# Attention's next queries: low part on GpSimd instead of VectorE, norm and rounding at other exponents on ScalarE

## The chip, the cores and the metric

The kernel runs on one core of one Trainium2 chip. The metric is the device time of one execution in microseconds (us). The change touches one of the kernel's stages, an attention over 32 tiles of queries.

## The reference, cut to what matters

The reference is a block of four layers on x (16 batches, 256 rows, 512 columns). The change lies in the third, a cross attention with keys and values from the context ctx_2048:

```
x = x + jnp.tanh(g_xattn[1]) * _L1_xattn_ref(_layernorm(x, axis=-1), ctx_2048, ctx_2048)

def _L1_xattn_ref(q, k, v):
    N_HEAD = 8
    b, d, m = q.shape
    qh = q.reshape(b * h, d // h, m)
    kh = k.reshape(b * h, d // h, -1)
    vh = v.reshape(b * h, c // h, -1)
    qk = jnp.einsum('bdm,bdn->bmn', qh, kh) * scale
    sm = jax.nn.softmax(qk, axis=-1)
    ret = jnp.einsum('bmn,bcn->bcm', sm, vh)
    return ret.reshape(b, c, m)
```

With d = 256 and 8 heads, each head has 32 features; scores are 512 x 512 per head. The query is the layer norm of a row of x, (x - mean) / sqrt(var + eps). Before this layer stand a convolution and a mixture of experts, behind it a second mixture of experts with a router that picks 2 of 8 experts.

## The kernel before, in words

The attention is cut into 32 units (UNITS). A unit is half a batch: 128 features, that is 4 heads (NH) of 32, against 512 positions. One pass of `body(j, i, u)` on each engine handles unit j. `unit_loop` (L1114) writes the first four and the last four units out and puts the others in a hardware loop of 4 units a trip; each engine has its own loop, and only semaphores tie them together.

For a unit, TensorE does each score twice. `score` (L1349) makes them with queries in the rows (into pA), and VectorE's `reduce` (L1710) takes the negated row maximum from them (into low). GpSimd's `halves` (L1291 to L1297) splits low into two parts, TensorE transposes them (`maxima`, L1368), ScalarE copies the result to tops (`keep`, L1561), and SyncE writes tops as two further rows of the query operand (`shift`, L1178 to L1182). `second` (L1371, matmul L1377) then makes the scores transposed with the maximum already subtracted, one 128 x 512 tile at a time, into pB, and ScalarE takes the exponent of each tile (L1608) into pt. A unit has 16 such tiles, so 16 score matmuls and 16 exponents. `values` (L1387) multiplies pt by the values, `sums` (L1400) adds up the denominators, for which GpSimd has added three of the four slices of pt (L1311, L1316).

The score matmuls of `second` use two banks in turn: `bank` picks one of pB's two, `place` numbers the tiles and leaves one place free for the transposes behind TURN = 10, and a tile waits until the one two places ahead has been read by ScalarE:

```
            def place(j, s, h):
                return NH * s + h + (1 if NH * s + h >= TURN and exists(j + 1) else 0)
            def second(j, u, s, h):
                n = place(j, s, h)
                if s == 0 and h == 0:
                    pe.wait_ge(s_md, 32 * j + 32)
                wait(pe, s_exp, made(j, n - 2))
```

The operands are kept in two parts, a rounded high one and a low one, the rest. For units ahead of time the kernel also makes the queries: ScalarE's `query` (L1590) applies the norm to a tile of x and writes nextq, `query_high` (L1596) rounds it into nexth, `query_low` (L1720, on VectorE) writes the difference nextl. SyncE's `store_query` (L1163, L1164) puts both parts in device memory, from where `load` (L1159) fetches them as operands of a later unit. In body j it is the query of unit j + 4. The query stands behind the exponent number 1 (counted from 0), the rounding behind number 5, the low part behind VectorE's reduce of beat 9. `query` waits until the low part before it is made, `query_high` until the stores before it have landed, `store_query` for the low part, and `load` of unit j + 3 for the stores of its query.

Other work of a unit: `add_row` (L1302) and `refine` (L1277 to L1286) on GpSimd, `scale` (L1716) and `measure` (L1724, L1727) on VectorE, `logarithm`, `inverse`, `root` and `norm` (L1566, L1571, L1577 and L1580, L1586) on ScalarE.

Of the kernel before, what the change touches and what calls it, by code (L numbers as in the profile page):

```python
# [6 lines left out]
F32R = mybir.dt.float32r  # L7
I32 = mybir.dt.int32
U32 = mybir.dt.uint32
ALU = mybir.AluOpType  # L10
# [14 lines left out]
NH, HD1 = 4, 32  # L25
# [46 lines left out]
def _build(nc, a, out, whole):  # L72
# [952 lines left out]
    with ExitStack() as st:  # L1025
# [85 lines left out]
        KHu, KLu, QHu, QLu = units(KH), units(KL), units(QH), units(QL)  # L1111
        QHr, QLr = (d.rearrange("b (th p) c -> (b th) p c", p=P) for d in (QH, QL))

        def unit_loop(eng, body):  # L1114

            trips = UNITS // TRIP
            for u in range(TRIP):
                body(u, 0, u)
            with eng.Fori(1, trips - 1) as i:
                for u in range(TRIP):  # L1120
                    body(i * TRIP + u, i, u)
            for u in range(TRIP):
                body(UNITS - TRIP + u, trips - 1, u)

        def exists(j):
            return not isinstance(j, int) or 0 <= j < UNITS
# [28 lines left out]
        def _(sp):  # L1155
            def load(j, u):
                for dst, src in ((ks[u][0:HD1], KHu[j]), (ks[u][HD1:2 * HD1], KLu[j]), (ks[u][2 * HD1:NS], KHu[j]),
                                 (qs[u][0:HD1], QHu[j]), (qs[u][HD1:2 * HD1], QHu[j]), (qs[u][2 * HD1:NS], QLu[j])):
                    sp.dma_start(dst, src).then_inc(s_ld[u], 16)  # L1159
# [24 lines left out]
            def body(j, i, u):  # L1184
                before, n = exists(j - 1), (u + TRIP - 1) % TRIP
                if exists(j + 3):
                    if before:
                        sp.wait_ge(s_b, made(j - 1, place(j - 1, CB - 1, NH - 1)))
                        sp.sem_inc(s_go, 1)
                        sp.wait_ge(s_qs, 32 * j)  # L1190
                    load(j + 3, n)
                if exists(j + 1):
                    shift(j + 1, (u + 1) % TRIP)
                if exists(j + 4):
                    store_query(j + 4)
                if exists(j - 2):
                    store(j - 2, (u + 2) % TRIP)
                if exists(j + 3):
                    if before:
                        sp.wait_ge(s_av, CB * j)  # L1200
                    load_values(j + 3, n)
                if exists(j - 4):
                    store_normed(j - 4)
# [42 lines left out]
        def _(pool):  # L1246
# [52 lines left out]
            def add_row(j):  # L1299
# [2 lines left out]
                pool.tensor_tensor(row, row, att, ALU.add).then_inc(s_x3, 1)  # L1302
                pool.wait_ge(s_x3, j + 1)

            def body(j, i, u):
                if exists(j + 1):
                    halves(j + 1, (u + 1) % TRIP)
                pool.wait_ge(s_exp, made(j, place(j, 1, NH - 1)))
                wait(pool, s_sum, 2 * j - 1)
                for n in range(2):  # L1310
                    pool.tensor_tensor(part_sum[:, 2 * n:2 * n + 2], pt[0][:, 2 * n:2 * n + 2], pt[1][:, 2 * n:2 * n + 2],  # L1311
                                       ALU.add).then_inc(s_add, 1)
                    pool.wait_ge(s_add, 4 * j + n + 1)
                pool.wait_ge(s_exp, made(j, place(j, 2, NH - 1)))
                for n in range(2):
                    pool.tensor_tensor(part_sum[:, 2 * n:2 * n + 2], part_sum[:, 2 * n:2 * n + 2], pt[2][:, 2 * n:2 * n + 2],  # L1316
                                       ALU.add).then_inc(s_add, 1)
                    pool.wait_ge(s_add, 4 * j + n + 3)
                if exists(j - 1):
                    add_row(j - 1)  # L1320
                if exists(j - 3):
                    refine(j - 3, (u + 1) % TRIP)

            halves(0, 0)
            constants()
            unit_loop(pool, body)
            add_row(UNITS - 1)
            for u in range(1, TRIP):
                refine(UNITS - TRIP + u, u)
# [223 lines left out]
        def _(act):  # L1553
# [44 lines left out]
            def body(j, i, u):  # L1598
                for s in range(CB):
# [5 lines left out]
                    for h in range(NH):  # L1605
                        n = place(j, s, h)
                        act.wait_ge(s_b, made(j, n))
                        act.activation(pt[s][:, h, :], bank(u, n), ACT.Exp, scale=SCALE1).then_inc(s_exp, 1)  # L1608
                        if NH * s + h == 1 and exists(j + 4):
                            query(j + 4)  # L1610
                        if NH * s + h == 5 and exists(j + 4):
                            query_high(j + 4)
                        if NH * s + h == 3 and exists(j - 3):
                            root(j - 3, (u + 1) % TRIP, 0)
                        if NH * s + h == 4 and exists(j - 3):
# [7 lines left out]
                        if NH * s + h == TURN + 2 and exists(j - 1):  # L1623
                            inverse(j - 1)

            keep(0, pB[1], 1)
            unit_loop(act, body)

            def columns(n):
                act.wait_ge(s_t, n + 1)  # L1630
# [71 lines left out]
        def _(dve):  # L1702
# [12 lines left out]
                wait(dve, s_x3, j)  # L1715
                dve.scalar_tensor_tensor(att, pO[u % 2], gates[:, 1:2], inv, ALU.mult, ALU.mult).then_inc(s_att, 1)  # L1716

            def query_low(j):
                dve.wait_ge(s_q, 2 * j - 6)
                dve.tensor_tensor(nextl.bitcast(F32R), nextq, nexth, ALU.subtract).then_inc(s_ql, 1)  # L1720

            def measure(j, u):
                dve.wait_ge(s_x3, j + 1)
                dve.bn_stats(stats6[:, u % 2, :], ap(XN, j * ROW, [[1, C]])).then_inc(s_bn, 1)  # L1724
# [6 lines left out]
            def body(j, i, u):  # L1731
                for beat in range(1, TILES, 2):
                    to = ahead(j, i, u, beat)
                    reduce(*to[:3], to[3] // 2)
                    if beat == 9 and exists(j + 4):
                        query_low(j + 4)
                    if beat == 5 and exists(j - 2):
                        measure(j - 2, (u + 2) % TRIP)
                    if beat == 13 and exists(j - 1):
                        scale(j - 1, u - 1)  # L1740
# [205 lines left out]
```

## Time and profile before

| what | value |
| --- | --- |
| median of 3 runs | 1681.53 us (1680.91 to 1683.77) |
| profiled execution | 1682.86 us |
| its span, first to last instruction | 1681.1 us |
| TensorE busy in the span | 1531.7 us, 91% |
| VectorE, ScalarE, GpSimd busy | 1250.4, 967.7 and 1021.2 us |
| the attention's 512 exponents (L1608) | 290.0 us busy |
| the 28 low parts (L1720) | first at 593.5, last at 1015.4 us |
| granted TensorE clock, mean | 0.951 |

Busy time is that of one engine; engines run beside each other, so the figures do not add up to the span. The span is a little shorter than the execution's time, since the latter has what lies around the first and the last instruction. A granted clock of 1.00 is TensorE's 2.4 GHz, 0.50 is 1.2 GHz.

### The profile page before, as it was taken

Reading aid. Unit: us, or ns where it says so; the run is one execution under the profiler, and the core shown is the slowest. Engines: PE = TensorE matmul, PEld = TensorE weight load, DVE = VectorE, ACT = ScalarE, POOL = GpSimd, SP = SyncE. Lnnn points to the kernel's source line nnn. Section 1 sums busy time; section 2 is a strip of 40 time slices with the busy share of each in tenths; the row PEclk is TensorE's granted clock in tenths of the full one; section 3 lists DMA queues with packets and bytes.
Section 4 is the critical chain, followed back from the end, with each engine's and each line's share of the span. In section 5 each row is a group of like instructions: output and inputs, shape, how many; then the busy total and the mean of one; then the engine's idle time right before and its main releaser. Section 6 shows DMA issues by size and latency. Waiting matters only on the chain.

```text
span 1681.1 us, 28191 instructions
## 1 busy us (share of the span) xinstructions
PE 1531.7 (91%) x8674; PEld 1054.5 (63%) x8674; DVE 1250.4 (74%) x1795; ACT 967.7 (58%) x1523; POOL 1021.2 (61%) x965
## 2 busy tenths in 40 slices
PE   5999999996676599999999999886999999999996
PEld 4677777775442244444444444366998999999985
DVE  7688888888538578888888887245677777777774
ACT  6333333325422167777778777745677676777763
POOL 4788888874203367887787787700355555555553
PEclk9999999998789589999999999987999999999998
DMA  6344444427452847677776764292244444444443
GB/s 248 114 139 139 143 140 142 137 102 202 100 154 72 194 118 191 184 181 190 189 184 180 197 186 133 70 331 102 51 76 76 76 79 81 80 76 76 76 77 50
DMA packets 110842, 224.24 MB, mean 133 GB/s; under 512 B 12704, under 2 KB 12704, under 8 KB 109856
## 3 DMA queue, kind: packets, MB, share of 16 engines
q1 hardware_dynamic: 94848, 185.88, 38.6%
q0 software_dynamic: 15904, 37.23, 12.7%
q8 instruction: 47, 0.77, 0.2%
q14 instruction: 43, 0.35, 0.1%
HBM read 146.71 MB, written 75.84 MB: 132 GB/s over the span
## 4 chain that ended last, share of the span: by engine, by line
PE 36%; DMA 23%; issue 3%; DVE 2%; ACT 1%; POOL 1%; SPq 0%; POOLq 0%; DVEq 0%; ACTq 0%
DMA out_rows<-XN,slots 21%; PE pB L1377 10%; PE pA L1359 8%; PE pO L1387 8%; PE pO L1400 4%; PE pO L1538 1%; DMA XN<-normed_rows,slots 1%; PE pO L1510 1%; PE pA L1527 1%; PE pB L1368 1%; PE pA L1449 1%; POOL out_rows L1343 1%; PE pB L1475 1%; PE pA L1456 1%; DVE low L1710 1%
## 5 line engine op out<-in xcount | busy, mean ns | idle before, releaser
L1710 DVE TENSOR_REDUCE low<-pA 128x2 f32<-128x1024 f32 x256 | 306.7, 1219 | 86.5 <-PE pA L1359 77.0
L1608 ACT ACTIVATE pt<-pB 128x512 f32<-128x512 f32 x512 | 290.0, 593 | 105.3 <-PE pB L1377 102.9
L430 PE MATMUL y<-kv,toep 128*128 128x288 f32 x1280 | 327.8, 413 | 9.0 <-DVEq L63 5.8
L1343 POOL DMA_INDIRECT out_rows<-XN,slots x71 | 196.8, 2772 | 216.0 <-DMA out_rows<-XN,slots 166.3
L430 PEld LDWEIGHTS y<-kv,toep 128*128 128x128 f32 x1280 | 239.1, 191 | 97.5 <-DVEq L63 34.1
L1527 PEld LDWEIGHTS pA<-XN,fc 128*128 128x128 f32 x2272 | 267.2, 193 | 7.7 <-ACT fc L1667 1.2
L1527 PE MATMUL pA<-XN,fc 128*128 128x128 f32 x2272 | 267.9, 277 | 1.7 <-DVE XN L1871 1.7
L1377 PE MATMUL pB<-qs,ks 98*128 98x512 f32 x512 | 229.1, 451 | 2.7 <-ACT pt L1608 2.4
L1377 PEld LDWEIGHTS pB<-qs,ks 98*128 98x128 f32 x512 | 97.0, 191 | 186.8 <-ACT pt L1608 121.9
L1359 PE MATMUL pA<-ks,qs 96*128 96x512 f32 x512 | 196.2, 428 | 19.5 <-DMA qs<-q_low 17.3
L400 ACT ACTIVATE ym<-y 128x384 f32<-128x384 f32 (+1 forms) x128 | 52.5, 410 | 230.7 <-PE y L430 230.7
L1672 ACT ACTIVATE proj_high<-WP 128x2048 fp32r x71 | 135.7, 1911 | 83.0 <-PE pO L1538 82.7
L1877 DVE TENSOR_TENSOR proj_low<-WP,proj_high 128x2048 fp32r<-128x2048 f32 x71 | 162.7, 2292 | 5.5 <-issue 1.6
L1311 POOL TENSOR_TENSOR part_sum<-pt 128x1024 f32<-128x1024 f32 x64 | 152.2, 2378 | 20.3 <-ACT pt L1608 12.9
L1316 POOL TENSOR_TENSOR part_sum<-part_sum,pt 128x1024 f32<-128x1024 f32 x64 | 159.5, 2493 | 7.1 <-POOL part_sum L1311 3.8
L1359 PEld LDWEIGHTS pA<-ks,qs 96*128 96x128 f32 x512 | 100.8, 199 | 59.8 <-DVE low L1710 27.9
L1667 ACT ACTIVATE fc<-WF 128x2048 f32 x71 | 134.5, 1895 | 4.0 <-DVEq L1866 4.0
L1387 PE MATMUL pO<-pt,vt 128*32 128x512 f32 x1024 | 136.8, 608 | 0.0
L368 POOL TENSOR_TENSOR R<-ym,qc 128x384 f32<-128x384 f32 (+1 forms) x128 | 99.2, 796 | 55.9 <-ACT ym L400 54.6
L151 POOL TENSOR_TENSOR kv<-kc 128x1024 f32<-128x1024 f32 x64 | 121.1, 1893 | 5.4 <-PEq L419 3.1
L1022 POOL DMA_INDIRECT XN<-normed_rows,slots x71 | 70.3, 991 | 85.5 <-DVEq L1866 63.2
L1538 PE MATMUL pO<-proj_high,hh 128*128 128x512 f32 x284 | 117.9, 415 | 3.5 <-DVE proj_low L1877 3.5
(262 smaller groups left out, 2443.6 us busy)
## 6 DMA issues: line engine op xcount, KB each, us to landing
ks<-ctx_high SPq DMA_DIRECT2D x64, 256.0 KB, 5.0
qs<-q_high SPq DMA_DIRECT2D x64, 256.0 KB, 7.0
kc<-in_ctx_conv SPq DMA_DIRECT2D x32, 384.0 KB, 5.5
XN<-in_x SPq DMA_DIRECT2D x16, 512.0 KB, 9.8
toep<-kernel_and_skip SPq DMA_DIRECT2D x32, 256.0 KB, 3.5
ct<-in_ctx SPq DMA_DIRECT2D x16, 512.0 KB, 6.7
ctx_high<-kh SPq DMA_DIRECT2D x16, 512.0 KB, 4.4
ctx_low<-kl SPq DMA_DIRECT2D x16, 512.0 KB, 5.2
```

Source lines behind the costliest of these rows:

```text
L430: m = pe.matmul(y[half].rearrange("p (l n) c -> p l n c", l=CB)[:, l, :, 0:PAIRS], toep[u][:, (l - s) * P:(l - s + 1) * P], kv[u][:, half, ...
L1311: pool.tensor_tensor(part_sum[:, 2 * n:2 * n + 2], pt[0][:, 2 * n:2 * n + 2], pt[1][:, 2 * n:2 * n + 2], ALU.add).then_inc(s_add, 1)
L1316: pool.tensor_tensor(part_sum[:, 2 * n:2 * n + 2], part_sum[:, 2 * n:2 * n + 2], pt[2][:, 2 * n:2 * n + 2], ALU.add).then_inc(s_add, 1)
L1343: pool.indirect_dma_start(out=out["out"], out_offset=bass.IndirectOffsetOnAxis(ap=slots[:, j:j + 1], axis=0), in_=ys[j % 2], in_offset=Non ...
L1359: m = pe.matmul(pA[n % 2][:, half, :], qs[u][0:NS, h, m0:m0 + P].bitcast(F32R), ks[u][0:NS, h, :].bitcast(F32R), start=True, stop=True)
L1377: pe.matmul(bank(u, n), ks[u][0:NS + 2, h, s * P:(s + 1) * P].bitcast(F32R), qs[u][0:NS + 2, h, :].bitcast(F32R), start=True, stop=True).t ...
L1387: m = pe.matmul(pO[u % 2][h * HD1:(h + 1) * HD1, :], vt[u][:, s, h * HD1:(h + 1) * HD1], pt[s][:, h, :], start=(s == 0), stop=(s == CB - 1))
L1527: m = pe.matmul(pH[j % 2][:, b * P:(b + 1) * P], fc[j % 2][:, k * C + b * P:k * C + b * P + P], xc[j % 2][:, k * P:(k + 1) * P], start=(k ...
L1608: act.activation(pt[s][:, h, :], bank(u, n), ACT.Exp, scale=SCALE1).then_inc(s_exp, 1)
L1672: act.activation(wph[j % 2].bitcast(F32R), ap(WP, e, [[1, CB * C]]), ACT.Copy).then_inc(s_w9, 1)
L1710: dve.tensor_reduce(ap(low[u % 2], t % CB * NH + t // CB, [[NH, 2], [1, 1]]), pA[n % 2], op=ALU.max, axis=AX.X, negate=True).then_inc(s_re ...
L1877: dve.tensor_tensor(wpl.bitcast(F32R), ap(WP, e, [[1, CB * C]]), wph[j % 2], ALU.subtract).then_inc(s_low, 1)
```

## The change

The low part moves from VectorE to GpSimd, where it stands at the end of a body and is that of unit j + 5. `query` and `query_high` now also handle unit j + 5; the query stands behind exponent number 8, the rounding behind number 13. The query of unit 4, which no body makes any more, is made ahead of the loops. SyncE stores a query before `shift` and not after it. `unit_loop` gets a number of trips to write out at the end, 2 for ScalarE and GpSimd, so that units 24 to 31 stand outside their loops.

```diff
-        def unit_loop(eng, body):
+        def unit_loop(eng, body, last=1):
...
-            with eng.Fori(1, trips - 1) as i:
+            with eng.Fori(1, trips - last) as i:
...
-            for u in range(TRIP):
-                body(UNITS - TRIP + u, trips - 1, u)
+            for j in range(UNITS - last * TRIP, UNITS):
+                body(j, j // TRIP, j % TRIP)
...
+                if exists(j + 4):
+                    store_query(j + 4)
                 if exists(j + 1):
                     shift(j + 1, (u + 1) % TRIP)
-                if exists(j + 4):
-                    store_query(j + 4)
...
+            def query_low(j):
+                pool.wait_ge(s_q, 2 * j - 6)
+                pool.tensor_tensor(nextl.bitcast(F32R), nextq, nexth, ALU.subtract).then_inc(s_ql, 1)
...
                 if exists(j - 3):
                     refine(j - 3, (u + 1) % TRIP)
-
+                if exists(j + 5):
+                    query_low(j + 5)
+
+            query_low(4)
             halves(0, 0)
             constants()
-            unit_loop(pool, body)
+            unit_loop(pool, body, 2)
...
-                        if NH * s + h == 1 and exists(j + 4):
-                            query(j + 4)
-                        if NH * s + h == 5 and exists(j + 4):
-                            query_high(j + 4)
+                        if NH * s + h == 8 and exists(j + 5):
+                            query(j + 5)
+                        if NH * s + h == 13 and exists(j + 5):
+                            query_high(j + 5)
...
+            query(4)
+            query_high(4)
             keep(0, pB[1], 1)
-            unit_loop(act, body)
+            unit_loop(act, body, 2)
...
-            def query_low(j):
-                dve.wait_ge(s_q, 2 * j - 6)
-                dve.tensor_tensor(nextl.bitcast(F32R), nextq, nexth, ALU.subtract).then_inc(s_ql, 1)
...
-                    if beat == 9 and exists(j + 4):
-                        query_low(j + 4)
```

In ScalarE's order, here in one unit of the loop, the place is that of exponents number 8 and 9 (`pt<-pB`), between the norm of an old row (`XN<-XN`) and the copy of the transposed maxima (`tops<-pB`). Before:

```order
L1586 ACTIVATE XN<-XN,shift_0,rstd_0 128x512
L1147 REGISTER_ALU
L1607 REGISTER_ALU
L1608 ACTIVATE pt<-pB 128x512
L1607 REGISTER_ALU
L1608 ACTIVATE pt<-pB 128x512
L1558 REGISTER_ALU
L1560 ISA
L1561 ACTIVATE tops<-pB 8x512
```

And in the changed kernel, whose lines have other numbers:

```order
L1147 REGISTER_ALU
L1614 REGISTER_ALU
L1615 ACTIVATE pt<-pB 128x512
L1147 REGISTER_ALU
L1597 ISA
L1597 REGISTER_ALU
L1597 ACTIVATE nextq<-XN,shift_of,root_of 128x512
L1614 REGISTER_ALU
L1615 ACTIVATE pt<-pB 128x512
L1565 REGISTER_ALU
L1567 REGISTER_ALU
L1568 ACTIVATE tops<-pB 8x512
```

The two exponents followed each other; now the query, with its wait for the low part before it, stands between them.

On SyncE's queue, behind the loads of a unit in the loop, the two stores of the query (`q_high`, `q_low`) stood behind the two rows written by `shift` (`qs<-tops`), which wait for ScalarE. Before:

```order
L1159 DMA qs<-q_low 32x4x512
L1179 ISA
L1182 DMA qs<-tops 1x4x512 x2
L1162 REGISTER_ALU
L1163 ISA
L1163 DMA q_high<-nexth 128x512
L1164 DMA q_low<-nextl 128x512
```

Changed:

```order
L1159 DMA qs<-q_low 32x4x512
L1162 REGISTER_ALU
L1163 ISA
L1163 DMA q_high<-nexth 128x512
L1164 DMA q_low<-nextl 128x512
L1179 ISA
L1182 DMA qs<-tops 1x4x512 x2
```

The stores now come first, and `shift` is queued behind their wait for the low part.

## Rows read from the trace of the kernel before

**Rows 1.** Busy time by window: us, each engine busy, PEclk, DMA share, GB/s.

```profile
583.68:593.24 9.56, 9.56 (x25) 5.88 (x24) 6.60 (x6) 6.84 (x12) 2.78 (x3) 0.50 0.52 106
...
608.55:1014.66 406.11, 405.43 (x2198) 177.16 (x2194) 350.47 (x314) 320.32 (x622) 325.56 (x279) 1.00 0.71 183
```

**Rows 2.** Waits, 615 to 1063 us: us in total, times, longest us.

```profile
PEld pB L1377 <- ACT pt L1608: 109.0, 179, 0.8
```

**Rows 3.** Timeline of TensorE's matmuls in one unit: start us, us, what, idle before.

```profile
841.81 0.50 PE L1377 MATMUL pB<-qs,ks 98*128 98x512 f32 x1
...
843.49 0.50 PE L1377 MATMUL pB<-qs,ks 98*128 98x512 f32 x1
...
847.53 0.49 PE L1377 MATMUL pB<-qs,ks 98*128 98x512 f32 x1
848.05 0.50 PE L1359 MATMUL pA<-ks,qs 96*128 96x512 f32 x1
...
857.37 0.50 PE L1377 MATMUL pB<-qs,ks 98*128 98x512 f32 x1
```

**Rows 4.** Timeline of ScalarE in the same unit and the start of the next.

```profile
842.35 1.08 ACT L1608 ACTIVATE pt<-pB 128x512 f32<-128x512 f32 x2 [0.34 <-PE pB L1377]
...
848.06 0.60 ACT L1608 ACTIVATE pt<-pB 128x512 f32<-128x512 f32 x1 [0.52 <-PE pB L1377]
...
850.49 1.09 ACT L1608 ACTIVATE pt<-pB 128x512 f32<-128x512 f32 x2 [1.07 <-PE pB L1377]
851.46 0.81 ACT L1590 ACTIVATE nextq<-XN,shift_of,root_of 128x512 f32 x1
852.16 0.60 ACT L1608 ACTIVATE pt<-pB 128x512 f32<-128x512 f32 x1
...
854.89 0.64 ACT L1596 ACTIVATE nexth<-nextq 128x512 fp32r<-128x512 f32 x1
```

**Rows 5.** The low part on VectorE: durations ns min/median/max of all; timeline of one.

```profile
L1720 DVE TENSOR_TENSOR nextl<-nextq,nexth x28: 2635/2659/2685, 593.5 to 1015.4; 128x512 fp32r<-128x512 f32 x28
...
844.18 2.67 DVE L1720 TENSOR_TENSOR nextl<-nextq,nexth 128x512 fp32r<-128x512 f32 x1
```

**Rows 6.** GpSimd: durations of all its row additions; timeline of the same unit.

```profile
L1302 POOL TENSOR_TENSOR XN<-XN,att x32: 1271/1282/1298, 618.3 to 1088.6; 128x512 f32 x24, 128x512 f32<-128x512 f32 x8
...
840.48 0.20 POOL L1294 CAST split<-low 128x16 fp32r<-128x16 f32 x1 [1.02 <-DVE low L1710]
...
841.48 4.83 POOL L1311 TENSOR_TENSOR part_sum<-pt 128x1024 f32<-128x1024 f32 x2 [0.49 <-ACT pt L1608]
```

**Rows 7.** Timeline of TensorE in units 28 and 29, which make no query.

```profile
1030.07 0.60 PE L1368 MATMUL pB<-ident,split 128*8 128x128 f32 x4
1030.43 0.47 PE L1377 MATMUL pB<-qs,ks 98*128 98x512 f32 x1
...
1043.99 0.50 PE L1377 MATMUL pB<-qs,ks 98*128 98x512 f32 x1
...
1045.26 0.60 PE L1368 MATMUL pB<-ident,split 128*8 128x128 f32 x4
```

**Rows 8.** Timelines of ScalarE and TensorE in unit 0, of TensorE in units 1, 2.

```profile
591.06 0.60 ACT L1608 ACTIVATE pt<-pB 128x512 f32<-128x512 f32 x1 [0.40 <-PE pB L1377]
591.92 0.60 ACT L1608 ACTIVATE pt<-pB 128x512 f32<-128x512 f32 x1 [0.26 <-PE pB L1377]
...
593.24 0.78 PE L1377 MATMUL pB<-qs,ks 98*128 98x512 f32 x1
...
610.31 0.49 PE L1377 MATMUL pB<-qs,ks 98*128 98x512 f32 x1
...
624.07 0.50 PE L1377 MATMUL pB<-qs,ks 98*128 98x512 f32 x1
```

**Rows 9.** Timeline of SyncE's issues behind a unit's loads.

```profile
837.20 0.38 SPq L1159 DMA_DIRECT2D qs<-q_low  x1
844.44 1.24 SPq L1182 DMA_DIRECT2D qs<-tops  x2
```

## The prediction

> **What bounds the kernel now.** I read the page, then the windows and waits of the attention stage, then one unit on each engine. Over the 406 us in which the attention loop runs at full clock TensorE is busy for 405.4 us [rows 1]. At 583.68 to 593.24, where the stage begins, the granted clock is 0.50, the 1.2 GHz level; afterwards it is 1.00, 2.4 GHz [rows 1]. So time is won or lost in this stage only if TensorE's queue gets through a unit sooner or later. The waits say who can hold it: the weight loads of its score matmuls stood behind ScalarE's exponents for 109.0 us [rows 2]. Much of that lies under matmuls already running, so the sum is no price; the order of events in a unit gives that.
>
> I number the exponents of a unit e0 to e15, and the score matmuls that feed them (L1377) pB0 to pB15. TensorE's start of pB8 to its start of pB10 takes 843.49 - 841.81 = **1.68 us**, from there to the next pB8 857.37 - 843.49 = **13.88 us** [rows 3]: 15.56 us a unit. Two facts matter.
>
> First, pB10 waits for e9. Score banks are a ring of two with one extra place for the transposes (place(10) is 11, and second() waits for made(j, 9)), so pB10 may not start before e9 has been read out. ScalarE's e8 and e9 are the row at 842.35 that lasts 1.08 us: e9 ends at 843.43 and pB10 starts at 843.49 [rows 3, 4]. TensorE has no slack there, and everything behind pB10 is in one queue.
>
> Second, VectorE's nextl (L1720) takes 2.64 to 2.69 us in all 28 cases [rows 5], for 512 elements a partition. It starts at 844.18, while GpSimd's two sums (L1311) run until 841.48 + 4.83 = 846.31, and ends at 846.85: it stands still until GpSimd's instruction is over and then needs 0.54 us [rows 5, 6]. The next reduce starts only then, and TensorE's pA matmul behind pB14 comes 848.05 - 847.53 = 0.52 us after it [rows 3, 5]. That gap belongs to the work that the change takes away. The Trainium skill has the same rule (SBUF — State Buffer, section Who interferes with whom): a VectorE instruction with two SBUF inputs and a GpSimd instruction that reads SBUF lock each other out for a whole instruction. By that rule, the trace agrees.
>
> **Part 1: nextl leaves VectorE.** The kernel shows itself what a unit costs without it. In unit 28 there is no further query to make: pB10 starts at 1030.43 and the next pB8 at 1043.99, 13.56 us [rows 7]. Against 13.88 us that is **-0.32 us a unit**. That stretch lacks ScalarE's two query instructions too, which is what the changed kernel has there, except for the rounding (part 3). Units 1 to 3 have 624.07 - 610.31 = 13.76 us before [rows 8], so they gain 0.20. From transposes to transposes, unit 28 to 29 took 1045.26 - 1030.07 = 15.19 us [rows 7] against 15.56, so 0.37 is the upper end of the gain and 0.20 the lower.
>
> A rule of the skill speaks against this. VectorE's price as this kernel pays it is 2.66 us, GpSimd's for a two-input operation of 128x512 is 1.28 us (L1302) [rows 5, 6]. The GPSIMD Engine Reference (section Elementwise — side-by-side cycle accounting) says that GpSimd needs 1.96 times VectorE's time for such an addition and that elementwise work belongs on VectorE; VectorE: DVE Perf Modes (its errata section) gives VectorE 691 ns for 512 elements. With only that leaving VectorE its reduces would hardly be early, and the sum would be +18.2 us instead of the one below. The rows decide otherwise: here VectorE's 2.66 us contain 2.1 us of standing still.
>
> **Part 2: the norm (query) between e8 and e9.** Before, it stood behind e1, where TensorE did not need e2 at once. Now it stands ahead of e9, which pB10 waits for. Where it is now behind e1, two exponents start at 850.49 and end at 851.58, the query starts at 851.46 and the next exponent at 852.16: the query pushes the following exponent by 852.16 - 851.46 = 0.70 us (its 0.81 less the overlap) [rows 4]. e8 itself cannot come sooner, since ScalarE was idle for 0.34 us before it, waiting for pB8 [rows 4]. So the first stretch becomes 1.68 + 0.70 = 2.38 us: **+0.70 us a unit**. Its bounds: the whole 0.81, and 0.49, the distance of two exponents that follow each other (1.08 less 0.59).
>
> **Part 3: the rounding (query_high) behind e13.** It takes 0.64 us, 0.54 after overlap. ScalarE idles for 0.52 us before e14, waiting for pB14, which itself comes 0.7 later [rows 4]; inverse and e13 are late by the same 0.7, so the gap stays and the rounding lies in it, within 0.02 us. I cost it at nothing; without that gap it would delay e14, and pB0 of the next unit waits for e14, over 1 us later.
>
> **Part 4: GpSimd.** It ends its unit at 839.46 and starts the halves at 840.48 and the sums at 841.48, having waited 1.02 and 0.49 us [rows 6]. The low part (1.28 us) fills the first wait, moves the halves by some 0.4 us to 841.4, and the transposes that need them stand right ahead of pB10 at 843.49 [rows 3]: hidden. The sums start at e7 as before or 0.1 us later and have no VectorE instruction against them any more. The query behind e8 needs the low part of the query before: done at about 840.9, wanted at 842.9, 2 us to spare. VectorE's statistics read one SBUF input and run beside it; I cost that at nothing, and even 0.7 us of delay there would lie beside the wait for e9.
>
> **Part 5: SyncE.** store_query moves ahead of shift. SyncE has issued its loads by 837.6 and shifts when tops is there, at 844.4 [rows 9]; the low part is ready at 840.9, so the two stores (each about 0.4 us of issue, like the load of 0.38 us in that row) go out between and delay nothing. Before, they stood behind the shift and behind nextl's end at 846.85, so they leave some 6 us earlier and the loads that wait for them have more room. The extra query ahead of the stage lies beside the first loads and the 16 score matmuls. The shortened loops of ScalarE and GpSimd put units 24 to 27 outside a loop; unit 28, whose 13.56 us I use, stands outside one already, so I cost that at nothing, 0.1 us either way in four units.
>
> **Sum.** Units 4 to 26: 23 x (0.70 - 0.32) = +8.7. Units 1 to 3: 3 x (0.70 - 0.20) = +1.5. Unit 0 at 1.2 GHz: e9 would start at 591.06 + 0.49 + 0.70 = 592.25 and end at 592.85, before pB10 at 593.24 [rows 8], so the query is hidden and some of the gain stays, -0.2. Unit 27 has no query and no low part: -0.3. Together **+9.7 us**. The profiled execution took 1682.86 us (span 1681.1), so 1692.6; it lies 1.3 us above the median of 1681.53, and from the median I forecast **1691.2 us**. With all bounds of the two prices at once the net is 0.49 - 0.37 = 0.12 to 0.81 - 0.20 = 0.61 us in 26 units, +3 to +16 us: 1684.6 to 1697.4.
>
> **Rivals.**
> 1. *Faster: the query is absorbed.* The place is pB10: if TensorE is not ready for it until 0.4 us or more behind today's moment, less than 0.32 us of the 0.70 reaches it and the gain wins. Unit 0 shows such a state: at the low clock e9 ended at 592.52 and pB10 started at 593.24, 0.72 us of room [rows 8]. With all absorbed, 27 x -0.32 = -8.6: 1672.9 us. Against it: in the loop pB10 follows e9 by 0.06 us [rows 3, 4].
> 2. *No change within 0.2%.* The gain is at its upper and the query's push at or below its lower end, the net 0.12 us or less: 26 x 0.12 = 3.1, 1684.6 us or a little under.
> 3. *No gain from VectorE.* The 13.56 us of unit 28 would then come from ScalarE's missing query, not from nextl, and the move to GpSimd would be worth nothing. The page GPSIMD Engine Reference of the Trainium skill, cited above, points this way. Then 26 x 0.70 = +18.2: 1699.7 us. Against it: TensorE's late matmul stands right behind the late reduce.
> 4. *GpSimd comes late.* If its low part ends later than 842.9, ScalarE stands before the query, and TensorE with it. Each us of that costs 26 us: 1717 us. It takes more than 2 us of delay; GpSimd's busy time is 325.6 of 406.1 us [rows 1], and 1.28 us in each of 26 units fits.
>
> **How the numbers follow.** My forecast 0.76, rival 1 0.07, rival 2 0.07, rival 3 0.05, rival 4 0.05. A measurement tells this kernel from no change at about 0.2%, 3.4 us: 1678.2 to 1684.9. So faster 0.07, same 0.07, slower 0.86. The range takes the forecast's bounds and a little of the run-to-run spread: 1684.5 to 1698, with about 2 in 10 outside.
>
> **What would show it.** Right: a unit of about 15.94 us; pB8 to pB10 2.38 us and still 0.05 us behind e9; pB10 to the next pB8 about 13.56; no 0.52 us gap behind pB14; nextl on GpSimd 1.2 to 1.3 us; its sums 2.38 us each; ScalarE never idle before the query for GpSimd. Wrong: pB10 well behind e9 with the query there (rival 1), a second stretch still at 13.88 (rival 3), or a wait of ScalarE for nextl (rival 4).

## The result and the profile after

| | before | changed |
|---|---|---|
| median, us | 1682.58 (4 runs, 1680.91 to 1683.77) | 1694.62 (4 runs, 1692.55 to 1698.44) |
| profiled execution, its span | 1682.86, 1681.1 | 1692.55, 1690.4 |
| ratio of the times, 95% interval | | 1.0075 [1.0052, 1.0098] |

The changed kernel is slower, by 12.0 us in the median. The forecast was 1692.6 us for the profiled execution (measured: 1692.55) and 1691.2 us for the median (measured: 1694.62); both measured times lie in its range of 1684.5 to 1698. First the windows, with the columns of [rows 1]: from pB8 of unit 1 to pB8 of unit 27, in the kernel before and then in the changed one.

```profile
608.55:1012.98 404.43, 403.75 (x2188) 176.02 (x2184) 349.15 (x313) 319.04 (x620) 323.88 (x279) 1.00 0.71 183
```

```profile
608.12:1021.88 413.76, 400.78 (x2188) 177.12 (x2184) 286.97 (x287) 319.16 (x620) 348.78 (x305) 1.00 0.71 180
```

The 26 units take 413.76 - 404.43 = 9.33 us longer. What is ahead of them is 0.4 us shorter and what follows is 0.4 longer (668.5 against 668.1), so this stretch holds the whole 9.3 us by which the spans differ. VectorE is busy for 62.2 us less, GpSimd for 24.9 more. TensorE now has gaps: 413.76 - 400.78 = 13.0 us, against 0.7.

One unit of the changed kernel on TensorE (start us, us, what, idle before), which answers to [rows 3]:

```profile
846.71 0.50 PE L1384 MATMUL pB<-qs,ks 98*128 98x512 f32 x1
...
848.00 0.60 PE L1375 MATMUL pB<-ident,split 128*8 128x128 f32 x4
849.08 0.50 PE L1384 MATMUL pB<-qs,ks 98*128 98x512 f32 x1 [0.49 <-ACT pt L1615]
...
853.11 0.50 PE L1384 MATMUL pB<-qs,ks 98*128 98x512 f32 x1
853.45 0.40 PE L1366 MATMUL pA<-ks,qs 96*128 96x512 f32 x1
...
862.58 0.50 PE L1384 MATMUL pB<-qs,ks 98*128 98x512 f32 x1
```

ScalarE in the same unit, which answers to [rows 4]:

```profile
847.25 0.60 ACT L1615 ACTIVATE pt<-pB 128x512 f32<-128x512 f32 x1 [0.34 <-PE pB L1384]
847.74 0.80 ACT L1597 ACTIVATE nextq<-XN,shift_of,root_of 128x512 f32 x1
848.45 0.58 ACT L1615 ACTIVATE pt<-pB 128x512 f32<-128x512 f32 x1
...
852.53 0.60 ACT L1615 ACTIVATE pt<-pB 128x512 f32<-128x512 f32 x1
853.01 0.64 ACT L1603 ACTIVATE nexth<-nextq 128x512 fp32r<-128x512 f32 x1
853.65 1.09 ACT L1615 ACTIVATE pt<-pB 128x512 f32<-128x512 f32 x2
```

Read the two together. e8 starts at 847.25, the query lies behind it, and e9 starts 1.20 us behind e8 instead of 0.49; it ends at 849.03, and pB10 starts at 849.08. TensorE, whose transposes were done 0.5 us earlier, stands still for just the time that the trace puts down to `pt`. pB8 to pB10 is 2.37 us, pB10 to the next pB8 862.58 - 849.08 = 13.50, together 15.87. Units 4 to 23 repeat this (once, in unit 6, e9 comes 0.10 later). pB14 (853.11) and the pA matmul behind it (853.45) now follow each other by 0.34 us and not by 0.52 as in [rows 3]; counted from pB10, pB15 comes 0.30 us sooner than before and pB2 of the next unit 0.40. The rounding stands between e13 and the pair e14 and e15 and ends at 853.65, just when e14 starts. That is 0.54 us behind pB14, the same distance as in the kernel before: the rounding fills the old gap and delays nothing.

The waits from 615 to 1000 us (us in total, times, longest), and then GpSimd's timeline in the unit shown above:

```profile
PE pB L1384 <- ACT pt L1615: 11.9, 24, 0.6
...
POOL part_sum L1320 <- ACT pt L1615: 13.7, 25, 0.7
```

```profile
844.32 1.27 POOL L1307 TENSOR_TENSOR nextl<-nextq,nexth 128x512 fp32r<-128x512 f32 x1 [0.19 <-POOL shift L1286]
845.55 0.19 POOL L1294 CAST split<-low 128x16 fp32r<-128x16 f32 x1
...
846.38 4.82 POOL L1315 TENSOR_TENSOR part_sum<-pt 128x1024 f32<-128x1024 f32 x2 [0.34 <-ACT pt L1615]
851.72 4.84 POOL L1320 TENSOR_TENSOR part_sum<-part_sum,pt 128x1024 f32<-128x1024 f32 x2 [0.52 <-ACT pt L1615]
```

TensorE's own wait for the exponents, 11.9 us in 24 cases, is the query between e8 and e9. GpSimd now stands idle for 0.34 and 0.52 us ahead of its sums, where before it waited 1.02 us for VectorE and 0.49 us for ScalarE [rows 6]: it has little to spare. That became important in the experiments. ScalarE never waits for the low part.

### The profile page after: what moved, and what is told of

Same layout as the page of the kernel before. It is cut to its first block, busy times and chain, and to the rows that moved or that the text cites. A ratio compares the mean times of both kernels' runs of the same rounds, so it can differ in the third digit from the quotient of the medians.

```text
span 1690.4 us, 28041 instructions
## 1 busy us (share of the span) xinstructions
PE 1527.3 (90%) x8674; PEld 1056.3 (62%) x8674; DVE 1184.1 (70%) x1767; ACT 968.6 (57%) x1523; POOL 1044.8 (62%) x993
## 4 chain that ended last, share of the span: by engine, by line
PE 33%; DMA 24%; issue 4%; ACT 3%; DVE 2%; POOL 1%; ACTq 0%; SPq 0%; POOLq 0%; DVEq 0%
DMA out_rows<-XN,slots 21%; PE pB L1384 10%; PE pO L1394 8%; PE pA L1366 6%; PE pO L1407 4%; DMA XN<-normed_rows,slots 2%; ACT pt L1615 1%; PE pO L1545 1%; PE pO L1517 1%; ACT nextq L1597 1%; PE pA L1456 1%; POOL out_rows L1350 1%; PE pA L1463 1%; PE pA L1534 1%; PE pB L1482 1%
## 5 line engine op out<-in xcount | busy, mean ns | idle before, releaser
L1350 POOL DMA_INDIRECT out_rows<-XN,slots x71 | 193.1, 2720 | 216.4 <-DMA out_rows<-XN,slots 177.3
L1366 PE MATMUL pA<-ks,qs 96*128 96x512 f32 x512 | 191.1, 419 | 18.8 <-DMA qs<-q_low 17.3
L1320 POOL TENSOR_TENSOR part_sum<-part_sum,pt 128x1024 f32<-128x1024 f32 x64 | 152.4, 2382 | 17.5 <-ACT pt L1615 14.4
```

The source lines that it names most:

```text
L1350: pool.indirect_dma_start(out=out["out"], out_offset=bass.IndirectOffsetOnAxis(ap=slots[:, j:j + 1], axis=0), in_=ys[j % 2], in_offset=Non ...
L1366: m = pe.matmul(pA[n % 2][:, half, :], qs[u][0:NS, h, m0:m0 + P].bitcast(F32R), ks[u][0:NS, h, :].bitcast(F32R), start=True, stop=True)
```

## The experiments

My theory was the prediction's: +0.70 us a unit from the query's place, less 0.32 to 0.38 from nextl's leaving VectorE. The rivals left were that the gain came from ScalarE and not from nextl (rival 3), and that something else than the query's place cost the 0.70. The runs of the kernel before in the same batches had medians of 1680.61, 1681.26, 1680.17 and 1678.96 us.

**Is the gain nextl's?** e1_low_first leaves ScalarE as it was before (query behind e1, rounding behind e5) and moves only the low part, to the start of GpSimd's body. From the kernel before:

```diff
             def body(j, i, u):
+                if exists(j + 4):
+                    query_low(j + 4)
...
-                    if beat == 9 and exists(j + 4):
-                        query_low(j + 4)
```

SyncE's `store_query` stands ahead of `shift`, as in the changed kernel.

> The kernel before with one thing changed: nextl is made by GpSimd at the start of its unit, ahead of the halves, for the same unit as before (j + 4); ScalarE's norm and rounding stay behind e1 and e5, SyncE stores ahead of the shift. My theory (the locked nextl on VectorE cost a unit 0.3 to 0.4 us, the query ahead of e9 cost 0.7): pB8 to pB10 stays 1.68 us, pB10 to the next pB8 falls from 13.88 to about 13.50 us, a unit takes 15.2 us, the kernel about 10 us less than before: 1672 us. Rival A (GpSimd is the engine that has too much to do, wherever ScalarE's work stands): the unit is as long as in the changed kernel, 15.87 us, 1690 us or more. Rival B (the gain in the second stretch came from the two ScalarE instructions that went away there, not from nextl): 13.88 us stays, the time is that of before within 2 us.

Measured: 1679.02 us, ratio 0.9992 [0.9975, 1.0008], span 1677.2, where I expected 1672 us. pB10 to the next pB8 fell to 13.49 us with ScalarE's two query instructions still in that stretch. So rival 3 falls: the gain is VectorE's. But only units 4 to 7 took 15.16 to 15.22 us. From unit 8 on pB8 to pB10 grew to 1.92 to 2.00 us, in the first unit of each trip of four to 2.3 from unit 12 on, and units 8 to 23 took 15.53 us in the mean. The wait was a new one, of the transposes for GpSimd's halves (waits, 740 to 960 us):

```profile
PEld pB L1374 <- POOL split L1296: 7.8, 14, 0.8
```

**Is the cost the query's place?** e2_query_behind_e9 moves the query one exponent on, e3_query_e13_high_e15 puts query and rounding behind e13 and e15. From the changed kernel:

```diff
-                        if NH * s + h == 8 and exists(j + 5):
+                        if NH * s + h == 9 and exists(j + 5):
                             query(j + 5)
```

> The changed kernel with the norm one exponent later, behind e9 instead of e8; nothing else moves, every engine has the same instructions. My theory (pB10 waits for e9 alone): the query now delays the copy of the maxima by about 0.2 us, for which pB11 has 0.5 us of room; pB8 to pB10 falls from 2.37 to 1.68 us, the second stretch stays at 13.5 to 13.6, a unit takes 15.2 to 15.3 us, and the kernel is about 17 us faster than the changed one, 1672 to 1678 us. Rival A (ScalarE or GpSimd simply has too much to do in this half of the unit): one place later changes less than 0.2 us a unit, the time stays at 1688 to 1695 us. Rival C (the maxima's copy is what the rest waits for): the first stretch falls but the second grows by as much, 15.8 us a unit.

> The changed kernel with the norm behind e13 and the rounding behind e15, in ScalarE's two longest gaps (0.52 us before e14, 1.07 us before the next e0). My theory: both are hidden, pB8 to pB10 is 1.68 us, the second stretch 13.5 us, 15.2 us a unit, 1672 to 1676 us, the same as with the norm behind e9 or 1 to 2 us better. Rival A (too much work for ScalarE or GpSimd, wherever it stands): 1688 us or more. Rival C (the rounding now comes too late for GpSimd, which then stands at the end of its unit): GpSimd waits for the rounding before nextl, and the unit grows by what it waits.

e2: 1675.96 us, ratio 0.9967 [0.9946, 0.9988]. e3: 1677.89, ratio 0.9978 [0.9958, 0.9999]. One number in one condition is worth 1.1%: with the query behind e9, pB8 to pB10 is back at 1.68 us. Yet both show what e1 showed, and e3 lies above the 1672 to 1676 us expected of it. Units 4 to 9 take 15.16 to 15.23 us, units 12 to 23 take 15.51 (e2) and 15.49 us (e3) in the mean. TensorE's transposes in e2:

```profile
824.31 0.60 PE L1375 MATMUL pB<-ident,split 128*8 128x128 f32 x4 [0.16 <-POOL split L1296]
...
839.78 0.60 PE L1375 MATMUL pB<-ident,split 128*8 128x128 f32 x4 [0.18 <-POOL split L1296]
```

And one turn of GpSimd in e3:

```profile
854.86 1.29 POOL L1307 TENSOR_TENSOR nextl<-nextq,nexth 128x512 fp32r<-128x512 f32 x1 [0.18 <-POOL shift L1286]
856.10 0.19 POOL L1294 CAST split<-low 128x16 fp32r<-128x16 f32 x1
...
856.84 4.84 POOL L1315 TENSOR_TENSOR part_sum<-pt 128x1024 f32<-128x1024 f32 x2 [0.25 <-ACT pt L1615]
861.83 4.84 POOL L1320 TENSOR_TENSOR part_sum<-part_sum,pt 128x1024 f32<-128x1024 f32 x2 [0.16 <-POOL part_sum L1315]
866.86 1.30 POOL L1302 TENSOR_TENSOR XN<-XN,att 128x512 f32 x1 [0.19 <-POOL part_sum L1320]
868.48 0.26 POOL L1277 TENSOR_SCALAR work<-mv,guess 128x1 f32<-128x1 f32 x1 [0.32 <-POOL XN L1302]
...
870.34 1.29 POOL L1307 TENSOR_TENSOR nextl<-nextq,nexth 128x512 fp32r<-128x512 f32 x1 [0.18 <-POOL shift L1286]
```

No idle time in this turn is over 0.32 us. The one ahead of the sums, which the view puts down to ScalarE, is 0.25 us in every unit of the loop from unit 5 on, so I read it as a fixed gap and not as a wait. All the others follow a step of GpSimd itself: 870.34 - 854.86 = 15.48 us is GpSimd's own work for a unit (15.49 us in the mean of units 12 to 23). GpSimd is the bound there, and TensorE cannot be faster than that however ScalarE is ordered. The first units escape since GpSimd starts the stage with room. In e3 it already takes 15.45 to 15.56 us a turn from unit 5 on, while the time from the end of its halves to the start of TensorE's transposes shrinks by some 0.3 us a unit: 1.27 us in unit 5, then 0.99, 0.72, 0.41 and, from unit 9 on, 0.06.

The bound is that of GpSimd's code inside its hardware loop. In e3's units 24 to 27 it stands outside:

```profile
978.38 1.29 POOL L1307 TENSOR_TENSOR nextl<-nextq,nexth 128x512 fp32r<-128x512 f32 x1
...
979.89 0.22 POOL L1296 TENSOR_TENSOR split<-low,split 128x16 fp32r<-128x16 f32 x1
980.19 4.83 POOL L1315 TENSOR_TENSOR part_sum<-pt 128x1024 f32<-128x1024 f32 x2
```

The instructions take as long as in the loop, but the gap ahead of the sums is 0.08 us, all gaps of a turn together come down from 1.95 to 1.42 us, and the turn to 14.93 us (units 25 and 26). From unit 25 on pB10 follows e9 by 0.05 us again. A GpSimd loop written out in full was not tried.

**Doses.** If GpSimd bounds e3, a second low part into a spare tile costs its full time; if the query's place bounds the changed kernel, a second norm behind e8 costs its full 0.70.

```diff
+                wait(act, s_spare, j - 4)
+                act.activation(spare, ap(XN, j * ROW, [[1, C]]), ACT.Identity, scale=ap(root_of, j, [[1, 1]]),
+                               bias=ap(shift_of, j, [[1, 1]])).then_inc(s_spare, 1)
```

> The changed kernel with the norm made twice behind e8, the first time into a spare tile: a clean dose for e9's delay, with no wait for a store as in the run before with both behind e8. My theory: e9 is pushed by 0.70 us once more, pB8 to pB10 goes from 2.37 to 3.07 us in units 1 to 26, the second stretch stays at 13.50 us, 16.57 us a unit, about 18 us above the changed kernel. Rival D (later stretches catch up): the second stretch shrinks below 13.4 us.

```diff
+                wait(pool, s_spare, j - 4)
+                pool.tensor_tensor(spare.bitcast(F32R), nextq, nexth, ALU.subtract).then_inc(s_spare, 1)
```

> The run with norm behind e13 and rounding behind e15 on GpSimd's low part, with the low part made twice, first into a spare tile: 1.28 us more for GpSimd. Theory (GpSimd is the bound of those runs at 15.46 us): the unit grows to 16.7 to 16.9 us, from the second or third unit on, about 33 us above that run. Rival E (something else is the bound at 15.46): GpSimd's slack takes a part, the unit grows by less than 1 us.

e5 and e8, like e4 and e11 below, were executed once each, so I read their stretches and not their totals. e5: 1708.95 us, span 1706.8, 16.4 over the changed kernel; units 1 to 26 alone take 18.1 more, where 26 x 0.70 is 18.2, and what is ahead of and behind them is 1.7 shorter. Its unit in TensorE's timeline:

```profile
839.56 0.50 PE L1386 MATMUL pB<-qs,ks 98*128 98x512 f32 x1
...
842.63 0.50 PE L1386 MATMUL pB<-qs,ks 98*128 98x512 f32 x1 [1.18 <-ACT pt L1620]
...
856.14 0.50 PE L1386 MATMUL pB<-qs,ks 98*128 98x512 f32 x1
```

The first stretch is 3.07 us, 0.70 more than in the changed kernel; the second is 13.51 as there. The dose acts on pB10 alone, in full. e8: 1707.49 us, span 1705.8, 29.7 over e3 (33 expected). Its transposes now wait openly for GpSimd:

```profile
823.37 0.60 PE L1379 MATMUL pB<-ident,split 128*8 128x128 f32 x4 [1.42 <-POOL split L1298]
...
840.15 0.60 PE L1379 MATMUL pB<-ident,split 128*8 128x128 f32 x4 [1.46 <-POOL split L1298]
```

From unit 6 to unit 23 GpSimd takes 16.74 us a turn (the two rows here are 16.78 apart), 15.46 + 1.28, and outside its loop 16.16. Both doses confirm their bound.

e4_both_behind_e8 was to be a third dose, with the rounding too behind e8.

```diff
-                        if NH * s + h == 13 and exists(j + 5):
+                        if NH * s + h == 8 and exists(j + 5):
                             query_high(j + 5)
```

> The changed kernel with the rounding directly behind the norm, so that both stand between e8 and e9: the suspected cost is made larger. My theory: the rounding pushes e9 by a further 0.54 us (0.64 less the overlap), pB8 to pB10 goes from 2.37 to 2.91 us, the second stretch stays at 13.5 us, a unit takes 16.4 us, and with 26 such units the kernel takes some 14 us more than the changed one, 1705 to 1709 us. Rival A (ScalarE's total work decides): no change, since ScalarE does the same work. Rival D (the delay of e9 is only partly passed on, TensorE or VectorE catches up later): the second stretch gets shorter by a part of the 0.54.

A miss: 1737.71 us, some 30 over what I expected. ScalarE shows a wait of another kind:

```profile
857.91 0.80 ACT L1597 ACTIVATE nextq<-XN,shift_of,root_of 128x512 f32 x1
859.16 0.63 ACT L1603 ACTIVATE nexth<-nextq 128x512 fp32r<-128x512 f32 x1 [0.45 <-DMA q_low<-nextl]
```

`nexth` may be written only once the stores of the previous query have landed, and these had been issued 1.5 us before the query. The wait (11.4 us in 22 cases) and the 0.54 us of the rounding itself explain about 25 us of the 45 over the changed kernel; the first stretches of units 1 to 26 are 28.1 us longer. The other 16.9 us lie in the second stretches of nine units that take 18.4 to 21.5 us. Two of the units, the long unit 4 and unit 6 (columns as in [rows 1]):

```profile
663.60:682.00 18.40, 16.83 (x88) 7.33 (x84) 11.08 (x12) 12.60 (x25) 13.45 (x13) 0.91 0.59 158
700.40:717.10 16.70, 15.37 (x88) 6.80 (x84) 11.03 (x12) 12.52 (x25) 13.46 (x13) 1.00 0.68 167
```

In all nine the granted clock is 0.83 to 0.91, in the other seventeen it is 1.00 and they take 16.6 to 17.1 us. In the longest, unit 3, TensorE stood still for 3.10 us before pB10, and pA matmuls behind it took 0.63 us where they take 0.40 in unit 6. What brought the clock down was not tested; unit 6, with a wait of 1.33 us, kept 1.00. It is no clean dose.

**VectorE without the lock.** Could the low part stay on VectorE, at a moment when GpSimd does not read? e6 puts it behind beat 3, e7 leaves it at beat 9 as before, both with e3's ScalarE order and SyncE's changed order. From e3:

```diff
-                if exists(j + 5):
-                    query_low(j + 5)
...
+                    if beat == 3 and exists(j + 4):
+                        query_low(j + 4)
```

> The low part is back on VectorE, but behind the reduce of beat 3, where GpSimd has only operations of 0.3 us; the norm is behind e13 and the rounding behind e15, GpSimd's loop has its old body. Theory (formed on the last runs): GpSimd with nextl has 15.46 us of work a unit and became the bound there after some 8 units; without it, and with no lock and nothing ahead of e9, no engine stands in TensorE's way: nextl takes 0.55 to 0.8 us, 15.17 us a unit to the end, some 8 us less than the runs with the low part on GpSimd and 9 to 10 us below the kernel before, about 1670 us. Rival E (the 15.46 us come from TensorE, SyncE or the transfers, which also run in these units): 15.46 us a unit from unit 8 on again, 1676 us. Rival F (VectorE is too busy for nextl anywhere): the second stretch is above 13.7 us.

> As the last, with the low part behind the reduce of beat 9, its place in the kernel before: VectorE has the same instructions, only one stands elsewhere. Theory of the lock: it meets GpSimd's sum again, takes 2.6 us, delays the next reduce and TensorE's matmul behind pB14, second stretch 13.8 to 13.9 us, 15.5 us a unit, 1679 to 1681 us, that is as the kernel before. Rival F (what counts is VectorE's load, not the meeting): no difference from the run with beat 3.

Both missed. e6: 1682.93 us, ratio 1.0015 [1.0004, 1.0026], unit 15.73. The lock is gone, but not the cost (tile row, then VectorE's timeline):

```profile
L1722 DVE TENSOR_TENSOR nextl<-nextq,nexth x28: 680/681/685, 585.3 to 1008.0; 128x512 fp32r<-128x512 f32 x28
```

```profile
833.55 1.23 DVE L1712 TENSOR_REDUCE low<-pA 128x2 f32<-128x1024 f32 x1 [0.92 <-PE pA L1359]
834.69 0.68 DVE L1722 TENSOR_TENSOR nextl<-nextq,nexth 128x512 fp32r<-128x512 f32 x1
835.29 1.22 DVE L1712 TENSOR_REDUCE low<-pA 128x2 f32<-128x1024 f32 x1
...
837.78 2.36 DVE L1712 TENSOR_REDUCE low<-pA 128x2 f32<-128x1024 f32 x2 [0.35 <-DVE mv L1729]
```

VectorE waits 0.92 us for TensorE before the reduce of beat 3, the first row, and not again until that of beat 11. The reduce right behind nextl, of beat 5, ends at 836.51; GpSimd's halves start at 836.78, and the transposes and pB10 hang on them. pB10 now comes 0.6 us behind e9, so even 0.6 us there is paid for. Also, the 128x1 `shift` of GpSimd that meets nextl takes 0.72 us instead of 0.26. The 681 ns agree with the 691 ns that the Trainium skill gives for such an addition of 512 elements (VectorE: DVE Perf Modes, its errata section).

e7: 1699.09 us, ratio 1.0115 [1.0098, 1.0131], unit 16.2. nextl is locked again (2.66 us), and in addition `shift` is queued on SyncE behind the store that waits for nextl. TensorE shows it:

```profile
828.80 0.49 PE L1377 MATMUL pB<-qs,ks 98*128 98x512 f32 x1 [0.65 <-DMA qs<-tops]
```

The next pair holds the order of the stores as it was before, and differs in one number, the beat of the low part.

```diff
-                    if beat == 9 and exists(j + 4):
+                    if beat == 1 and exists(j + 4):
                         query_low(j + 4)
```

> As the last, with the low part behind beat 9, its place in the kernel before: one instruction of VectorE stands elsewhere, nothing else differs. In the earlier run of this kind SyncE's stores stood ahead of the shift, so the shift waited for nextl and TensorE for the shift, 0.65 us a unit. Theory of the lock: nextl takes 2.6 us, the second stretch is 13.8 to 13.9 us, a unit 15.5 to 15.6 us, as in the kernel before: 1679 to 1683 us. Rival F (load, not lock): the same as with beat 1. If the store order did not matter: 16.2 us a unit as in the earlier run.

> The low part on VectorE behind the reduce of beat 1, norm behind e13, rounding behind e15, SyncE's stores behind the shift as in the kernel before. What the runs have taught: behind beat 3 nextl was not locked (0.68 us) but stood in the one part of the unit in which VectorE has no slack (beat 3 to beat 9), and the unit took 15.73 us. Before beat 3 VectorE waits 0.9 us for TensorE. Theory: nextl meets GpSimd's row addition, waits for at most its end, takes 0.7 to 1.3 us, delays the next reduce by 0.1 to 0.4 us at most; GpSimd has 14.2 us of work a unit; nothing stands ahead of e9. 15.17 to 15.3 us a unit, 1671 to 1675 us, below both kernels. Rival F (VectorE's total load): 15.7 us again, 1682 us. Rival G (the lock makes it 2 us and more here too): 15.4 to 15.6 us.

e10: 1677.96 us, ratio 0.9990 [0.9976, 1.0005], unit 15.55, nextl 2.66 us: ScalarE's late query alone is worth nothing (15.56 us a unit before), and against e7 the order of two issues on SyncE is worth 0.65 us a unit. e9: **1670.20 us, ratio 0.9937 [0.9912, 0.9961]**, faster than both kernels. VectorE in e9:

```profile
828.54 1.23 DVE L1712 TENSOR_REDUCE low<-pA 128x2 f32<-128x1024 f32 x1 [0.90 <-PE pA L1359]
829.69 1.15 DVE L1722 TENSOR_TENSOR nextl<-nextq,nexth 128x512 fp32r<-128x512 f32 x1
830.76 2.34 DVE L1712 TENSOR_REDUCE low<-pA 128x2 f32<-128x1024 f32 x2
```

Behind beat 1 GpSimd is in a single addition (829.00, 1.28 us) and no longer in its sums, so nextl stands still for some 0.5 us (1.32 us is the longest of the 28), and VectorE has just waited 0.90 us, so most of the delay costs nothing. Not all: in units 7 to 23 nextl takes about 1.15 and 1.30 us in turn. Where it takes 1.15, pB8 to pB10 is 1.68 to 1.70 us and the unit about 15.2; where it takes 1.30, they are 1.81 to 1.86 and about 15.35, against 15.56 before. Unit 5 alone takes 16.70 us: there the rounding waited 1.78 us for the landing of q_low, and TensorE 1.06 us behind it.

How much of the gain is this? Units 1 to 26 take 399.2 us in e9's profile, 5.2 less than in the kernel before. Its span (1663.2) is shorter by 18.0, for two other reasons: pB8 of unit 1 comes 4.7 us sooner and what follows unit 27's pB8 is 8.1 shorter. Ahead of unit 1 the clock differs. From 575 to 590 us, e9 and then e10:

```profile
575.00:590.00 15.00, 13.35 (x34) 7.53 (x34) 11.38 (x12) 5.92 (x11) 4.54 (x23) 0.64 0.82 182
```

```profile
575.00:590.00 15.00, 14.35 (x32) 8.77 (x32) 10.85 (x9) 6.07 (x11) 4.14 (x19) 0.50 0.71 153
```

In e10 the granted clock is still at the 1.2 GHz level all through, in e9 it has gone to 2.4 GHz on the way. Behind unit 27 there is a dip of the clock, and the 20 us from 120 us behind its pB8 have 0.61 in e9 where they have 0.53 in the kernel before. Whether that is rule or luck is open: of e9's six executions two have a mean clock of 0.958 (the profiled one is among them) and four 0.951 to 0.954, and of the 17 of the kernel before one has 0.958. But it does not make the difference of the medians. With 0.951 to 0.954 e9 takes 1669.74 to 1672.64 us, the kernel before 1676.92 to 1684.78 (15 executions, median 1680.26); with 0.958 it is 1662.83 and 1664.86 against 1673.07. So the stage explains 5.2 of the 10.0 us between the medians, and the rest is open. The cleanest price of the place is the pair that differs in nothing else: e9's median lies 7.8 us below e10's, and its units 1 to 26 are 5.7 us shorter.

**The rest of the change.** e11 takes back only SyncE's order in the changed kernel; e12 is the changed kernel once more.

```diff
-                if exists(j + 4):
-                    store_query(j + 4)
                 if exists(j + 1):
                     shift(j + 1, (u + 1) % TRIP)
+                if exists(j + 4):
+                    store_query(j + 4)
```

> The changed kernel with SyncE's two stores behind the shift again. The stores then go out at about 1.4 us after the shift's start, land 2.3 us later and reach ScalarE about 1 us after it wants to round: nexth waits for a landing, e14 starts up to 1 us later, pB0 of the next unit up to 0.1 us later. Theory: 15.9 to 16.1 us a unit, 0 to 5 us above the changed kernel, and a wait of ScalarE's nexth for the transfer of q_low that the changed kernel has not. Rival: no such wait, 15.87 us: then the order on SyncE's queue was no part of the effect.

> The changed kernel once more, unedited, in more rounds. Its first four runs lie 12 us above the kernel before in the median, its profiled execution 9.7 us, and the two traces differ by 8.7 us at the end of the attention stage. My theory (the stage's 8.7 us are all of it, the rest is spread between executions): the ratio to the kernel before is 1.0055 to 1.0065. If instead something outside the stage costs 2 to 3 us more in most executions, the ratio stays at 1.0070 to 1.0080.

e11: 1692.95 us, span 1690.8, unit 15.87. The rounding now waits for the landing of q_low (9.5 us in 14 cases, 740 to 960 us), in a gap, at no cost. So the new order is neither cost nor gain here. e12: 1692.68 us (6 runs, 1685.92 to 1697.95), ratio 1.0079 [1.0055, 1.0103], again with units of 15.87. My theory (1.0055 to 1.0065) missed; the ratio is the one expected if something outside the stage costs 2 to 3 us more. The medians differ by 12.0 and 13.7 us in the two measurements, the spans of the first two traces by 9.3. The granted clock does not explain it: with a mean of 0.951 or 0.952 both kernels still lie some 13 us apart. The 0.4 us by which the time outside the span is longer (2.15 against 1.76) is a small part. The other 2 to 4 us are open, as are those of e9. Part of them may be which execution was profiled: that of the kernel before, 1682.86 us, lies 3.9 us above the median of 1678.96 that e12 is compared with. Traces of several executions of both kernels would be the next step.

## Why the prediction was right

- **Bound, pB10 behind e9.** Right: in all of units 1 to 26 pB10 starts 0.05 us behind e9, and e5 doubles the price exactly. Rival 1 (the query absorbed) would have needed a TensorE that comes later than that; it happened only in unit 0, at 1.2 GHz, where the forecast had it.
- **Part 1, nextl leaves VectorE.** Right in mechanism: e1 has the gain with ScalarE unchanged, and e9 against e10 (15.27 and 15.55 us a unit in units 6 to 23) has 0.28 us of it from nextl's place alone. The size: -0.38 in the loop, not -0.32, and just beyond the 0.37 that I gave as the upper end. Unit 28, from which I took 13.56, stands outside the loops, where a stretch is about 0.08 us longer (below), so it understated the gain. Rival 3 fell with e1. The rule of the Trainium skill behind it (GPSIMD Engine Reference, Elementwise — side-by-side cycle accounting) gives 1.96 times VectorE's time for 2048 elements a partition. Here, with 512, the addition takes 1.277 us on GpSimd and 0.681 on VectorE unlocked, 1.88 times, and the best kernel of this study (e9) has it on VectorE. What decided here was VectorE's locked 2.66 us.
- **Part 2, +0.70.** Exact: 1.675 to 2.373 us. The Trainium skill says that activations that follow each other overlap by some 93 ns (ScalarE: Activation LUTs, What ACT_TABLE_LOAD costs); here the query of 0.81 us pushes by 0.70, 0.11 less.
- **Part 3, rounding at nothing.** Right, within the 0.02 us stated: e14 starts 0.54 us behind pB14 with the rounding ahead of it and without. It rests on pB14's being late too, as the prediction has it.
- **Part 4, GpSimd at nothing.** Right for this kernel, and rival 4's wait never appeared. But 1.28 us "fit" in the busy time of a unit only because the unit is 15.87. I did not add up GpSimd's instructions with the gaps between them: 15.49 us. Of the 0.70 us that the query's place costs only 0.38 a unit can be had back in the loop while nextl is on GpSimd, as e2 and e3 show.
- **Units 24 to 26, costed at the loop's price.** This term was mis-sized, and so was unit 28 as a yardstick. Outside the loops e8 starts 0.62 us behind pB8 and not 0.54, and pB10 to the next pB8 is 13.58 and not 13.50: 16.04 us a unit.
- **The sum.** Units 1 to 3: +1.47 us (forecast 1.5). Units 4 to 23: +6.40 (forecast 20 x 0.38 = 7.6). Units 24 to 26: +1.46 (forecast 3 x 0.38 = 1.1). Units 0 and 27: -0.1 and -0.2 (forecast -0.2 and -0.3). The two sizes that were off cancel in part: 9.3 us of span where 9.7 stood. The prediction has the clock at 1.00 behind 593.24 us; it stayed at 0.50 until about 597, and no term hung on that.
- **The median** lies 3.4 us above the forecast, though the profiled execution is within 0.1 of it. That closeness is luck: the span rose by 9.3 us and the time outside it by 0.4, which no term of the sum had, and the profiled execution was the shortest of the four. Of the 3.4 us, 1.05 are that the kernel before had a median of 1682.58 in this comparison and not 1681.53. The trace explains the profiled execution; the other 2.3 us are open.

## What to carry to other kernels

Before anything is put ahead of an instruction on an engine, find out which later instruction of the bounding engine waits for just that one: one exponent further on, the same norm cost nothing where it had cost 0.70 us a unit. An instruction that suffers from a lock need not change its engine; look first for a place in its own engine's order where there is slack and the other engine reads little (e9), since a move to the other engine (e1 to e3) makes that one the next bound. So add up each engine's work for one turn, its fixed gaps included, before moving work onto it, and distrust the first turns of a loop, which run on saved room.

## What the chip showed unexpectedly

- The lock works both ways: 0.72 instead of 0.26 us for a 128x1 operation of GpSimd that meets VectorE's nextl (e6), besides 2.66 instead of 0.68 us for nextl under GpSimd's sums.
- GpSimd, whose turn is some 0.3 us longer than TensorE's, did not hold it up before unit 8 (e1) or 9 (e2, e3), and then did in full.
- The same GpSimd code has gaps of 1.95 us a turn inside its hardware loop and of 1.42 outside (e3), and 15.49 us a turn become 14.93.
- Units whose ScalarE code stands outside its hardware loop have e8 0.08 us later behind pB8, in the kernel before too (0.62 in units 1 to 3, 0.54 in the loop), and e0 likewise. For ScalarE the loop's code is thus the quicker one, for GpSimd the slower. Why was not tried.
